# Second expert stage of a four-layer kernel: gelu kept in PSUM, the guard read from PSUM by VectorE, the expert sum on GpSimd in three of four chunks

## The chip, the cores and the metric

The kernel runs on one core of a Trainium2 chip. The time is device microseconds (us) of one execution. Three executions of the kernel before took 1536.53, 1538.46 and 1542.48 us; the median, 1538.46 us, is the figure to be compared. One more execution was taken with the hardware profiler.

## The reference

Four layers run one behind the other on 2 x 1024 = 2048 tokens of width 128, each an attention part and a feed-forward part with a residual and a layer norm around each. The change lies in the last feed-forward part, a mixture of 8 experts of which 2 are weighted for each token:

```python
scores = jax.nn.softmax(inputs @ Wr + br, axis=-1)
_, top_idx = jax.lax.top_k(scores, K)                 # K = 2 of E = 8
mask = jax.nn.one_hot(top_idx, E).sum(-2)
weights = jax.nn.softmax(jnp.where(mask > 0, scores, -jnp.inf), axis=-1)
hid = jax.nn.gelu(jnp.einsum('btc,ecd->bted', inputs, W1) + b1, approximate=False)   # DFF = 512
expert_out = jnp.einsum('bted,edc->btec', hid, W2) + b2
expert_out = jnp.where(jnp.isnan(expert_out), 0.0, expert_out)
return jnp.einsum('bte,btec->btc', weights, expert_out)
```

The line with `isnan` is the guard: a NaN of an expert's output counts as zero. The kernel gets this from max and min against zero (or against the value), which leave every other number as it is. After this part, `x = x + layernorm(...)` gives the output.

## The kernel before

Each of the five engines has one program, written out in order; semaphores hold them together. Nothing is scheduled by a planner: an instruction waits at its place, and everything behind it on its engine waits too. Activations lie transposed, features on the 128 partitions and tokens along the free axis, in four chunks of 512 tokens (`NC = 4`, `CH = 512`).

The second expert stage ("stage 7" in the names) runs over 128 steps: chunk c = i // 32 and m = i % 32, where m counts the quarters (128 hidden features) of the eight experts, four quarters to an expert. I call the four steps of an expert in a chunk a group, n = i // 4, so there are 32 groups, eight in a chunk. fp32 accuracy comes from splitting each number into a rounded part and a rest and multiplying three ways, so every product costs three matmuls. At its loop index i, each engine does this:

- TensorE (`pe_moe7`): three matmuls of the first product of step i into one of four PSUM banks (L2036 to L2038), then three matmuls of the second product of step i - 4 (`LAG7 = 4`; L2042, L2043, L2045). The second products of a group add up in PSUM bank 3 or 4, by turns. Before the first matmul of a group n goes into that bank, TensorE waits until what read group n - 2 out of it is done (semaphore "ye").
- ScalarE (`act_moe7`): gelu of step i from PSUM into an SBUF buffer GE7 (L2485, "ge"), then the rounded copy of step i - 1 (L2491, "hi"); every fourth index the finished group out of its bank with the bias added, into YE7 (L2497, "ye").
- VectorE (`dve_moe7`): the rest of step i, gelu minus its rounded copy (L2560, "lo"), and then one of four stations of group n, station k at index i = 4n + 9 + k. They are the guard's max (L2536, "ca"), its min and sum (L2541, "cb"), the weighting with the token weights (L2549, "cc") and the sum over experts (L2552, "acc").
- GpSimd: splits the weights into the two parts in chunk 0 (L2003, L2005), forms the rests of the stage's input (L2031), and does the small norm steps.
- SyncE: brings the token weights of each group in, broadcast to all partitions.

Beside the steps stand other pieces at fixed (c, m): four feature blocks and their products of the attention before (chunk 0), norm, turning and routing of the second half of the tokens (chunk 1, `dve_route7_*`, `act_route7`), and the final norm of finished chunks (`dve_end` and its parts in chunks 2 and 3).

Names to follow: `hm` counts first products, `w2` second products; `RING7 = 5` buffers hold the rounded part and the rest. In the trace KS and SHARED are SBUF memory (GE7 lies in both), ROUNDED is SBUF with rounded numbers, PS is PSUM.

Of the kernel before, what the change touches and what calls it, by code (L numbers as in the profile page):

```python
# [2993 lines left out]
```

## Time and profile before

| | |
|---|---|
| median of three executions | 1538.46 us |
| the profiled execution | 1548.84 us, its span 1547.0 us |
| mean granted TensorE clock | 0.886 of full speed |
| busy over the span | TensorE 1269.9 us (82%), VectorE 1174.2 (76%), ScalarE 1118.9 (72%), GpSimd 278.8 (18%) |
| second expert stage | first step at 1301.3 us, last first product at 1527.7, end of the span 1547.0 |

The profiled execution is slower than the median by 10.4 us; durations and positions below are its own. A row of a window tells what an engine was busy with, and "idle before" what it waited for. Matmuls overlap in the pipeline: each lasts 0.39 us in the trace, though in the stage's steps they start every 0.23 us at the full clock, so TensorE's pace is read from starts.

### The profile page before, as it was taken

How to read it: one execution, taken by the hardware profiler on the slowest of the kernel's cores; microseconds unless marked ns; L12 is line 12 of the kernel's file. 1: busy time of each engine (PE TensorE's matmuls, PEld its weight loads, DVE VectorE, ACT ScalarE, POOL GpSimd, SP SyncE). 2: the span in 40 equal slices, each digit the busy share in tenths (PEclk: the TensorE clock that was granted, in tenths of full speed). 3: DMA queues.
4: the chain of work that ended last, by engine and by line, in shares of the span. 5: the costliest groups of instructions: out<-in, count | busy, mean ns of one | idle time of the engine just before them, and what ended most of it. 6: DMA issues, size and time to landing. Idle time of an engine off the chain costs nothing.

```text
span 1547.0 us, 22272 instructions
## 1 busy us (share of the span) xinstructions
PE 1269.9 (82%) x8010; PEld 645.8 (42%) x8010; DVE 1174.2 (76%) x2121; ACT 1118.9 (72%) x1584; POOL 278.8 (18%) x377
## 2 busy tenths in 40 slices
PE   6699999986777777777777787788899988788996
PEld 3334444452111111111111145556667766576874
DVE  7878886367697797966669556668978797876898
ACT  4267787658999999999999733455565655967985
POOL 2500002451000000002000034444011035621000
PEclk9589999995788778888788897999999998999998
DMA  5300100004000000100000020013233234001111
GB/s 186 109 23 24 44 24 4 1 11 140 0 21 21 1 21 1 36 21 1 21 1 0 29 116 0 1 25 89 91 99 99 80 103 151 21 28 35 42 48 55
DMA packets 41086, 70.47 MB, mean 46 GB/s; under 512 B 6416, under 2 KB 14864, under 8 KB 40208
## 3 DMA queue, kind: packets, MB, share of 16 engines
q1 hardware_dynamic: 40976, 69.05, 14.5%
q8 instruction: 63, 1.03, 0.3%
q14 instruction: 47, 0.39, 0.1%
HBM read 59.26 MB, written 9.76 MB: 45 GB/s over the span
## 4 chain that ended last, share of the span: by engine, by line
PE 37%; DVE 24%; ACT 20%; issue 13%; POOL 3%; DMA 1%; SPq 1%; DVEq 0%; ACTq 0%; POOLq 0%
ACT SHARED L1134 12%; PE PS L823 5%; DVE SHARED L1170 4%; PE PS L1048 4%; PE PS L1035 3%; PE PS L787 3%; DVE KS L2218 3%; PE PS L645 2%; PE PS L1349 2%; PE PS L712 2%; ACT ROUNDED L2142 2%; PE PS L2036 2%; PE PS L2038 2%; PE PS L2037 1%; PE PS L2045 1%
## 5 line engine op out<-in xcount | busy, mean ns | idle before, releaser
L1134 ACT ACTIVATE SHARED<-PS 128x1536 f32<-128x1536 f32 (+1 forms) x346 | 458.4, 1432 | 34.2 <-PE PS L1035 32.8
L1035 PE MATMUL PS<-QS,KS 48*128 48x512 bf16 (+1 forms) x1006 | 237.2, 461 | 123.4 <-ACT SHARED L1134 118.9
L1170 DVE TENSOR_TENSOR SHARED<-SHARED 128x1536 f32<-128x1536 f32 (+1 forms) x170 | 276.5, 1700 | 45.8 <-ACT SHARED L1134 45.8
L803 ACT ACTIVATE SHARED<-PS 128x512 f32<-128x512 f32 (+3 forms) x384 | 163.8, 493 | 75.4 <-PE PS L791 65.9
L1035 PEld LDWEIGHTS PS<-QS,KS 48*128 48x128 bf16 (+1 forms) x1006 | 40.5, 99 | 365.8 <-ACT SHARED L1134 337.9
L1048 PE MATMUL PS<-SHARED,Vg 128*16 128x512 f32 x1024 | 157.3, 692 | 5.2 <-DVE SHARED L1170 5.1
L2036 PE MATMUL PS<-ROUNDED 128*128 128x512 f32 x328 | 135.8, 414 | 6.2 <-ACT KS L2154 6.2
L732 DVE TENSOR_REDUCE NM<-PS 128x2 f32<-128x1024 f32 (+3 forms) x128 | 124.4, 1019 | 16.0 <-PE PS L718 13.7
L2038 PE MATMUL PS<-ROUNDED 128*128 128x512 f32 x328 | 130.3, 397 | 0.0
L2037 PE MATMUL PS<-ROUNDED 128*128 128x512 f32 x328 | 130.2, 397 | 0.0
L2142 ACT ACTIVATE ROUNDED<-KS 128x512 fp32r<-128x512 f32 x100 | 63.1, 631 | 90.2 <-DVE KS L2218 90.1
L328 POOL TENSOR_SCALAR VEY<-MVY 128x4 f32<-128x4 f32 x32 | 8.9, 279 | 611.2 <-DVE MVY L269 610.5
L2045 PE MATMUL PS<-ROUNDED 128*128 128x512 f32 x228 | 94.1, 413 | 28.2 <-DVE ROUNDED L2200 16.1
L2560 DVE TENSOR_TENSOR ROUNDED<-KS,ROUNDED 128x512 fp32r<-128x512 f32 x103 | 75.1, 732 | 32.1 <-ACT ROUNDED L2491 31.2
L823 PE MATMUL PS<-SHARED,Vg 128*16 128x256 f32 (+3 forms) x1152 | 93.6, 399 | 6.4 <-issue 4.8
L2042 PE MATMUL PS<-ROUNDED 128*128 128x512 f32 x228 | 91.5, 401 | 8.2 <-ACT ROUNDED L2491 4.4
L478 POOL COPY Vg<-XH 128x256 f32<-128x256 f32 x16 | 9.1, 572 | 485.8 <-PE PS L1048 291.4
L2485 ACT ACTIVATE KS<-PS,C 128x512 f32<-128x512 f32 x103 | 71.1, 690 | 27.6 <-PE PS L2038 26.5
L2043 PE MATMUL PS<-ROUNDED 128*128 128x512 f32 x228 | 90.1, 395 | 0.0
L712 PE MATMUL PS<-SHARED 48*128 48x512 bf16 (+3 forms) x384 | 79.3, 364 | 12.8 <-DVE NM L732 6.8
L787 PE MATMUL PS<-SHARED 50*128 50x512 bf16 (+3 forms) x384 | 84.0, 343 | 4.4 <-ACT SHARED L803 2.8
L2200 DVE TENSOR_TENSOR ROUNDED<-KS,ROUNDED 128x512 fp32r<-128x512 f32 x100 | 75.0, 750 | 11.9 <-ACT ROUNDED L2142 7.4
(276 smaller groups left out, 2371.9 us busy)
## 6 DMA issues: line engine op xcount, KB each, us to landing
SHARED<-wx SPq DMA_DIRECT2D x64, 256.0 KB, 3.2
SHARED<-in_moe SPq DMA_DIRECT2D x3, 1600.0 KB, 10.7
SHARED<-wx SPq DMA_DIRECT2D x16, 224.0 KB, 3.0
SHARED<-kx SPq DMA_DIRECT2D x32, 96.0 KB
KS<-kx SPq DMA_DIRECT2D x32, 96.0 KB
SHARED<-wx SPq DMA_DIRECT2D x16, 192.0 KB, 2.9
SHARED<-wx SPq DMA_DIRECT2D x16, 160.0 KB, 2.8
qx<-SHARED SPq DMA_DIRECT2D x16, 128.0 KB, 2.4
```

Source lines behind the costliest of these rows:

```text
L712: ins = pe.matmul(PS[:, slot(k, x):slot(k, x) + n], q[r, p, qt * P:qt * P + P], key[r, p, hi * CH:hi * CH + n], start=True, stop=not diag)
L732: dve.tensor_reduce(out=dst, in_=src, axis=AX.X, op=ALU.max, negate=True).then_inc(A[0, "a_red"], 1)
L787: ins = pe.matmul(bank(at, q0), K0[g % 3][r, p, kt * P:kt * P + P], Q0[g % 3][r, p, qh * CH + q0:qh * CH + CH], start=True, stop=not diag)
L803: act.activation(PB[t % 3][:, h, q0:CH], bank(RING0[n % 3], q0), ACT.Exp, scale=SCORE_SCALE)\
L823: ins = pe.matmul(PS[32 * h:32 * h + VC, 6 * CH + a:6 * CH + b], Vg[g % 2][:, kt, h, :], PB[t % 3][:, h, a:b], start=kt == 0, stop=last an ...
L1035: ins = pe.matmul(bank((v % 2) * GRP + f - a), KS[g % 2][r, h // 2, kt * P:kt * P + P], QS[g % 2][r, h // 2, qh * CH:(qh + 1) * CH], start ...
L1048: ins = pe.matmul(PS[32 * h:32 * h + VC, 6 * CH:7 * CH], Vg[g % 2][:, kt, h, :], EX[:, f * CH:f * CH + CH], start=kt == 0, stop=kt == KT - 1)
L1134: act.activation(dst, PS[:, (v % 2) * GRP * CH:((v % 2) * GRP + b - a) * CH], ACT.Exp if second == qh else ACT.Sigmoid, scale=SCORE_SCALE)\
L1170: dve.tensor_tensor(ex_tile(j), ex_tile(j), GR[w % RING][:, 0:(b - a) * CH], ALU.mult)\
L2036: pe.matmul(dst, w[0], x[0], start=start, stop=False)
L2037: pe.matmul(dst, w[0], x[1], start=False, stop=False)
L2038: return pe.matmul(dst, w[1], x[0], start=False, stop=stop)
```

## The change

Four edits, all in this stage:

1. The gelu is written back into the PSUM bank it came from, and the rounded copy (ScalarE) and the rest (VectorE) read it there. The buffers GE7 are gone. TensorE now gets a first-product bank back when the rest is formed ("lo") and no longer when the gelu is done ("ge").
2. ScalarE's copy of the finished group with its bias (YE7) is gone. VectorE's two guard instructions read the bank directly and add the bias themselves: max(y + b, 0), then min(y + b, that).
3. So TensorE gets a second-product bank back from the second guard instruction ("cb") of group n - 2.
4. In chunks 1 to 3 the weighting and the sum over experts are done on GpSimd (`pool_moe7`), in chunk 0 still on VectorE. The two rests of the input (`pool_rest_of_h`) and the root of the final norm (`pool_y`) stand between them.

```diff
         def pool_from_moe5(pool, pw):
...
-            for c in range(2, 4):
-                pool_rest_of_h(pool, 7, c)
-            for c in range(NC):
-                pool_y(pw, edges["end"], c)
+            pool_moe7(pool, pw)
...
             # pe_moe7, second(i): n, k = divmod(i, 4)
                 pe.wait_ge(A[7, "hi"], i + 1)
                 if k == 0:
                     if n >= 2:
-                        pe.wait_ge(A[7, "ye"], n - 1)
+                        pe.wait_ge(A[7, "cb"], n - 1)
...
                     if i >= len(HM7):
-                        pe.wait_ge(A[7, "ge"], i - len(HM7) + 1)
+                        pe.wait_ge(A[7, "lo"], i - len(HM7) + 1)
...
         def act_moe7(act):
-            for i in range(N7 + 5):
+            for i in range(N7 + 1):
                 c, m = divmod(i, M7)
                 if i < N7:
                     act.wait_ge(A[7, "hm"], i + 1)
-                    if i >= RING7:
-                        act.wait_ge(A[7, "lo"], i - RING7 + 1)
-                    act.activation(GE7[i % RING7], bank(HM7[i % len(HM7)]), ACT.Gelu, bias=col("eb1", m)).then_inc(A[7, "ge"], 1)
+                    act.activation(hidden_bank7(i), hidden_bank7(i), ACT.Gelu, bias=col("eb1", m)).then_inc(A[7, "ge"], 1)
                 if 1 <= i < N7 + 1:
...
-                    act.activation(HG7[n % RING7], GE7[n % RING7], ACT.Copy).then_inc(A[7, "hi"], 1)
-                if i % 4 == 0 and 8 <= i:
...
-                    act.activation(YE7[n % 2], bank(3 + n % 2), ACT.Identity, bias=col("eb2", n % E3))\
-                       .then_inc(A[7, "ye"], 1)
+                    act.activation(HG7[n % RING7], hidden_bank7(n), ACT.Copy).then_inc(A[7, "hi"], 1)
...
+        def weigh7(eng, n):
+            c, e = divmod(n, E3)
+            eng.wait_ge(A[7, "cb"], n + 1)
+            eng.wait_ge(*weights_landed7(n))
+            if n >= 2:
+                eng.wait_ge(A[7, "acc"], summed(n - 1))
+            dst = chunk(ACC7, c) if e == 0 else CC7
+            eng.tensor_tensor(dst, CB7, WB7[n % len(WB7)], ALU.mult).then_inc(A[7, "cc"], 1)
+
+        def gather7(eng, n):
+            c, e = divmod(n, E3)
+            eng.wait_ge(A[7, "cc"], n + 1)
+            eng.tensor_tensor(chunk(ACC7, c), chunk(ACC7, c), CC7, ALU.add).then_inc(A[7, "acc"], 1)
+
+        def pool_moe7(pool, pw):
+            for n in range(E3, E3 * NC):
+                weigh7(pool, n)
+                if n % E3:
+                    gather7(pool, n)
+                if n in (E3 + 1, E3 + 2):
+                    pool_rest_of_h(pool, 7, n - E3 + 1)
+                if n in (17, 18, 25):
+                    pool_y(pw, edges["end"], (17, 18, 25).index(n))
+            pool_y(pw, edges["end"], 3)
...
             # dve_moe7, station(n, k)
-                    dve.tensor_scalar(CA7, YE7[n % 2], 0.0, None, ALU.max).then_inc(A[7, "ca"], 1)
+                    dve.tensor_scalar(CA7, bank(3 + n % 2), col("eb2", e), 0.0, ALU.add, ALU.max)\
+                       .then_inc(A[7, "ca"], 1)
...
-                    dve.scalar_tensor_tensor(out=CB7, in0=YE7[n % 2], scalar=0.0, in1=CA7,
-                                             op0=ALU.min, op1=ALU.add).then_inc(A[7, "cb"], 1)
...
+                    dve.scalar_tensor_tensor(out=CB7, in0=bank(3 + n % 2), scalar=col("eb2", e), in1=CA7,
+                                             op0=ALU.add, op1=ALU.min).then_inc(A[7, "cb"], 1)
+                elif c == 0 and k == 2:
+                    weigh7(dve, n)
+                elif c == 0 and e:
+                    gather7(dve, n)
...
-                    dve.tensor_tensor(HL7[k], GE7[k], HG7[k].bitcast(F32), ALU.subtract).then_inc(A[7, "lo"], 1)
+                    dve.tensor_tensor(HL7[k], hidden_bank7(i), HG7[k].bitcast(F32), ALU.subtract).then_inc(A[7, "lo"], 1)
```

What stands in each engine's row: first TensorE at the last index of chunk 3 that begins a group's second products, before. S7_ge, S7_ye, S7_hi and S7_lo are the semaphores named above.

```order
L2036 MATMUL PS<-ROUNDED 128x512 [waits S7_ge]
L2037 MATMUL PS<-ROUNDED 128x512
L2038 MATMUL PS<-ROUNDED 128x512
L2042 MATMUL PS<-ROUNDED 128x512 [waits S7_ye,S7_hi]
L2043 MATMUL PS<-ROUNDED 128x512
L2045 MATMUL PS<-ROUNDED 128x512 [waits S7_lo]
```

The same place in the change:

```order
L2036 MATMUL PS<-ROUNDED 128x512 [waits S7_lo]
L2037 MATMUL PS<-ROUNDED 128x512
L2038 MATMUL PS<-ROUNDED 128x512
L2042 MATMUL PS<-ROUNDED 128x512 [waits S7_cb,S7_hi]
L2043 MATMUL PS<-ROUNDED 128x512
L2045 MATMUL PS<-ROUNDED 128x512 [waits S7_lo]
```

TensorE's instructions and their order are the same; only two of its waits are for other semaphores.

Then VectorE over one group in chunk 3, before: four rests, and a station behind each.

```order
L2560 TENSOR_TENSOR ROUNDED<-KS,ROUNDED 128x512 [waits S7_w2,S7_hi]
L2536 TENSOR_SCALAR SHARED<-SHARED 128x512 [waits S7_cb,S7_ye]
L2560 TENSOR_TENSOR ROUNDED<-KS,ROUNDED 128x512 [waits S7_w2,S7_hi]
L2541 SCALAR_TENSOR_TENSOR SHARED<-SHARED 128x512 [waits S7_cc,S7_ca]
L2560 TENSOR_TENSOR ROUNDED<-SHARED,ROUNDED 128x512 [waits S7_w2,S7_hi]
L2549 TENSOR_TENSOR SHARED<-SHARED 128x512 [waits S7_acc,w5_in2,S7_cb]
L2560 TENSOR_TENSOR ROUNDED<-KS,ROUNDED 128x512 [waits S7_w2,S7_hi]
L2552 TENSOR_TENSOR SHARED<-SHARED 128x512 [waits S7_cc]
```

The same in the change, where L2569 is the rest, L2550 and L2556 the guard, C the columns with the biases:

```order
L2569 TENSOR_TENSOR ROUNDED<-PS,ROUNDED 128x512 [waits S7_w2,S7_hi]
L2550 TENSOR_SCALAR SHARED<-PS,C 128x512 [waits S7_cb,S7_w2]
L2569 TENSOR_TENSOR ROUNDED<-PS,ROUNDED 128x512 [waits S7_w2,S7_hi]
L2556 SCALAR_TENSOR_TENSOR SHARED<-PS,C,SHARED 128x512 [waits S7_cc,S7_ca]
L2569 TENSOR_TENSOR ROUNDED<-PS,ROUNDED 128x512 [waits S7_w2,S7_hi] x3
```

The guard kept its places in VectorE's row, each behind the rest of its step; the stations for the weighting and the sum are gone.

Last GpSimd's row where the final norm of chunks 0 and 1 begins in the change (weighting L2522, sum L2527):

```order
L2522 TENSOR_TENSOR SHARED<-SHARED 128x512 [waits S7_acc,w5_in0,S7_cb]
L2527 TENSOR_TENSOR SHARED<-SHARED 128x512 [waits S7_cc]
L328 TENSOR_SCALAR VEY<-MVY 128x4 [waits y_var]
L329 TENSOR_TENSOR RSY<-VEY,ROOT 128x4 [waits pw_own]
L2522 TENSOR_TENSOR SHARED<-SHARED 128x512 [waits S7_acc,w5_in2,S7_cb]
L2527 TENSOR_TENSOR SHARED<-SHARED 128x512 [waits S7_cc]
```

Before, L328 and L329 stood there alone; now each pair waits behind the weighting and the sum of a group.

## Rows read from the trace of the kernel before

**Rows 1.** Windows, the stage's four chunks: start:end, length, busy (count), clock, DMA share, GB/s
```profile
core 0: us, PE busy (x) PEld busy (x) DVE busy (x) ACT busy (x) POOL busy (x), PEclk, DMA share, GB/s
1301.30:1371.70 70.40, 59.80 (x247) 44.28 (x246) 49.66 (x79) 57.35 (x97) 33.42 (x33) 0.96 0.10 30
1371.70:1436.80 65.10, 53.92 (x223) 41.35 (x222) 47.96 (x136) 48.65 (x81) 16.99 (x20) 0.92 0.11 33
1436.80:1484.20 47.40, 45.43 (x201) 36.60 (x200) 42.70 (x92) 41.88 (x74) 3.20 (x4) 1.00 0.14 40
1484.20:1527.60 43.40, 42.91 (x191) 35.21 (x190) 39.80 (x78) 40.21 (x71) 1.60 (x2) 1.00 0.16 49
```
**Rows 2.** One line, first products of the stage: count, ns min/median/max, first and last start
```profile
L2036 PE MATMUL PS<-ROUNDED x128: 387/389/799, 1301.3 to 1527.7; 128*128 128x512 f32 x128
```
**Rows 3.** Timeline, an undisturbed group of chunk 3: start, duration, engine, line, operation, names
```profile
1493.74 0.39 PE L2036 MATMUL PS<-ROUNDED 128*128 128x512 f32 x1
1494.62 0.69 ACT L2485 ACTIVATE KS<-PS,C 128x512 f32<-128x512 f32 x1
1495.10 0.39 PE L2036 MATMUL PS<-ROUNDED 128*128 128x512 f32 x1
1495.21 0.62 ACT L2491 ACTIVATE ROUNDED<-KS 128x512 fp32r<-128x512 f32 x1
1495.78 0.39 PE L2042 MATMUL PS<-ROUNDED 128*128 128x512 f32 x1
1495.86 0.69 DVE L2560 TENSOR_TENSOR ROUNDED<-KS,ROUNDED 128x512 fp32r<-128x512 f32 x1 [0.17 <-ACT ROUNDED L2491]
...
1496.47 0.69 DVE L2541 SCALAR_TENSOR_TENSOR SHARED<-SHARED 128x512 f32<-128x512 f32 x1
```
**Rows 4.** Timeline, a wait of TensorE for VectorE in chunk 2
```profile
1476.63 0.39 PE L2043 MATMUL PS<-ROUNDED 128*128 128x512 f32 x1
1478.38 0.50 PE L2045 MATMUL PS<-ROUNDED 128*128 128x512 f32 x1 [1.36 <-DVE ROUNDED L2560]
1478.72 0.40 PE L2036 MATMUL PS<-ROUNDED 128*128 128x512 f32 x1
...
1477.64 0.68 DVE L2560 TENSOR_TENSOR ROUNDED<-KS,ROUNDED 128x512 fp32r<-128x512 f32 x1
```
**Rows 5.** One line each, ScalarE's rounded copies: count, ns min/median/max, first and last start
```profile
L2491 ACT ACTIVATE ROUNDED<-KS x103: 612/630/672, 1304.9 to 1529.7; 128x512 fp32r<-128x512 f32 x103
...
L373 ACT ACTIVATE ROUNDED<-PS x8: 588/591/618, 1022.3 to 1401.3; 128x512 fp32r<-128x512 f32 x8
```
**Rows 6.** One line each, VectorE and GpSimd while weights are split, 1280 to 1300
```profile
L2218 DVE TENSOR_TENSOR KS<-SHARED,PS x7: 674/678/682, 1281.4 to 1296.5; 128x512 f32<-128x512 f32 x7
...
L2200 DVE TENSOR_TENSOR ROUNDED<-KS,ROUNDED x8: 686/882/1750, 1280.8 to 1297.9; 128x512 fp32r<-128x512 f32 x8
...
L2005 POOL TENSOR_TENSOR ROUNDED<-SHARED,ROUNDED x4: 1262/1438/1799, 1288.2 to 1299.5; 128x512 fp32r<-128x512 f32 x4
```
**Rows 7.** One line, VectorE's rests, 1318 to 1341 (chunk 0)
```profile
L2560 DVE TENSOR_TENSOR ROUNDED<-KS,ROUNDED x9: 676/1092/1772, 1317.8 to 1340.9; 128x512 fp32r<-128x512 f32 x9
```
**Rows 8.** Timeline, GpSimd and TensorE in chunk 1
```profile
1387.80 1.74 POOL L340 TENSOR_SCALAR XN<-X,NMX,RSX 128x128 f32<-128x128 f32 x4
...
1392.28 5.00 POOL L340 TENSOR_SCALAR XN<-X,NMX,RSX 128x128 f32<-128x128 f32 x4
...
1397.33 1.12 PE L399 MATMUL PS<-ident,XN 128*128 128x128 f32 x4 [3.47 <-POOL XN L340]
...
1399.10 0.63 PE L2038 MATMUL PS<-ROUNDED 128*128 128x512 f32 x1
1399.53 0.63 PE L2042 MATMUL PS<-ROUNDED 128*128 128x512 f32 x1
```
**Rows 9.** Waits, 1436.8 to 1528 (chunks 2 and 3): who <- whom, us, times, longest
```profile
PE PS L2045 <- DVE ROUNDED L2560: 2.4, 3, 1.4
```
**Rows 10.** Timeline, a turning on TensorE and a norm's statistics on VectorE in chunk 2
```profile
1457.25 0.60 PE L2051 MATMUL PS<-ident,SHARED 128*128 128x128 f32 x4
1457.61 0.47 PE L2036 MATMUL PS<-ROUNDED 128*128 128x512 f32 x1
...
1464.10 0.89 DVE L266 BATCH_NORM_STATS2 STY<-PS 128x6 f32<-128x128 f32 x4
1465.02 0.38 DVE L269 BATCH_NORM_AGGREGATE MVY<-STY 128x2 f32<-128x6 f32 x4
```
**Rows 11.** Windows, the expert stage before, 1140 to 1160
```profile
1140.00:1160.00 20.00, 17.04 (x75) 13.32 (x74) 14.70 (x25) 13.77 (x24) 0.00 (x0) 1.00 0.30 87
```
**Rows 12.** Timeline, the end of the last group
```profile
1531.74 0.50 PE L2045 MATMUL PS<-ROUNDED 128*128 128x512 f32 x1
1532.28 0.69 ACT L2497 ACTIVATE SHARED<-PS,C 128x512 f32<-128x512 f32 x1 [1.43 <-PE PS L2045]
...
1537.35 0.69 DVE L2552 TENSOR_TENSOR SHARED<-SHARED 128x512 f32<-128x512 f32 x1
1538.10 1.11 PE L2051 MATMUL PS<-ident,SHARED 128*128 128x128 f32 x4 [5.86 <-DVE SHARED L2552]
```

More of the change, by code:

```diff
@@ L2301, in pool_split7 @@
             pool_split_weights(pool, 7, 2 * e + 1, M3B[:, k], M3BH[:, k], M3BL[:, k])
-        for nm in ("hm", "ge", "hi", "lo", "w2", "ye", "ca", "cb", "cc", "acc", "lgs"):
+        for nm in ("hm", "ge", "hi", "lo", "w2", "ca", "cb", "cc", "acc", "lgs"):
             A[7, nm] = sem(f"S7_{nm}")
@@ L2308, in sandwich @@
         HM7 = (0, 1, 2, 5)
-        GE7 = [spare[:, 512 * i:512 * i + 512] for i in range(4)] + [arena(2560, 512)]
         HG7 = [rounded(512 * i, 512) for i in range(RING7)]
         HL7 = [work_rounded(512 * i, 512) for i in (0, 1, 2, 3, 9)]
-        YE7 = [work(2048 + 512 * i, 512) for i in range(2)]
         CA7 = work(3072, 512)
@@ L2432, in pe_moe7 @@
                     if i >= len(HM7):
-                        pe.wait_ge(A[7, "ge"], i - len(HM7) + 1)
+                        pe.wait_ge(A[7, "lo"], i - len(HM7) + 1)
                     at = slice(m * P, m * P + P)
-                    pe_parts(pe, bank(HM7[i % len(HM7)]), (M3AH[:, at], M3AL[:, at]), (chunk(hR, c), chunk(HTL[7], c)),
+                    pe_parts(pe, hidden_bank7(i), (M3AH[:, at], M3AL[:, at]), (chunk(hR, c), chunk(HTL[7], c)),
                              True, True).then_inc(A[7, "hm"], 1)
@@ L2476, in pe_beside_moe7, with hidden_bank7 @@
                 pe_turn_y(pe, edges["end"], 2, ACC7, A[7, "acc"], summed(3 * E3 - 1))
+        def hidden_bank7(i):
+            return bank(HM7[i % len(HM7)])
         def act_moe7(act):
-            for i in range(N7 + 5):
+            for i in range(N7 + 1):
                 c, m = divmod(i, M7)
@@ L2531, in station @@
                 if k == 0:
-                    dve.wait_ge(A[7, "ye"], n + 1)
+                    dve.wait_ge(A[7, "w2"], 4 * n + 4)
                     if n:
                         dve.wait_ge(A[7, "cb"], n)
-                    dve.tensor_scalar(CA7, YE7[n % 2], 0.0, None, ALU.max).then_inc(A[7, "ca"], 1)
+                    dve.tensor_scalar(CA7, bank(3 + n % 2), col("eb2", e), 0.0, ALU.add, ALU.max)\
+                       .then_inc(A[7, "ca"], 1)
                 elif k == 1:
@@ L2540, in station @@
                         dve.wait_ge(A[7, "cc"], n)
-                    dve.scalar_tensor_tensor(out=CB7, in0=YE7[n % 2], scalar=0.0, in1=CA7,
-                                             op0=ALU.min, op1=ALU.add).then_inc(A[7, "cb"], 1)
-                elif k == 2:
-                    dve.wait_ge(A[7, "cb"], n + 1)
-                    dve.wait_ge(*weights_landed7(n))
-                    if n >= 2:
-                        dve.wait_ge(A[7, "acc"], summed(n - 1))
-                    dst = chunk(ACC7, c) if e == 0 else CC7
-                    dve.tensor_tensor(dst, CB7, WB7[n % len(WB7)], ALU.mult).then_inc(A[7, "cc"], 1)
-                elif e:
-                    dve.wait_ge(A[7, "cc"], n + 1)
-                    dve.tensor_tensor(chunk(ACC7, c), chunk(ACC7, c), CC7, ALU.add).then_inc(A[7, "acc"], 1)
+                    dve.scalar_tensor_tensor(out=CB7, in0=bank(3 + n % 2), scalar=col("eb2", e), in1=CA7,
[4 more added lines that the diff above has]
+                    gather7(dve, n)
             for i in range(N7 + 9):
```

4 lines of the change are left out of this document (removed).

## The prediction, on record before the changed kernel ran

> **What bounds the kernel now.** I read the windows of the stage first, since all edits lie in it. Each chunk has 32 steps of six matmuls. Undisturbed, a step takes 1.36 us, as two first products in a row show (1493.74 and 1495.10, [rows 3]), 0.23 a matmul, so 32 steps take 43.5 us. Chunk 3 takes about that, and chunk 2 takes 47.4 [rows 1]: TensorE sets the pace there and the others keep up. Chunks 0 and 1 take 70.4 and 65.1: TensorE stands waiting for ScalarE and VectorE, which have the attention pieces, the norms and the routing beside the steps. Then I read the waits of chunks 2 and 3: TensorE's for the rests add up to 2.4 us [rows 9]. So relief for ScalarE and VectorE is worth next to nothing in the second half of the stage, and a new wait of TensorE is paid there in full.
>
> Last I read the timeline of one undisturbed group, for how far each engine lies behind TensorE [rows 3]. First product 103 starts at 1493.74 and its gelu 0.88 later. The rounded copy of step 102 follows at 1495.21, the rest of step 102 at 1495.86, and the guard's second instruction at 1496.47; it ends at 1497.16. That instruction belongs to group 23, because "cb" of group n' stands behind the rest of step 4n' + 10.
>
> **The new wait, and its price.** In the change the first matmul of group n's second products waits for "cb" of group n - 2. TensorE issues it at its index 4n + 4. "cb" of n - 2 stands in VectorE's row behind the rest of step 4n + 2. That rest needs rounded copy 4n + 2, which stands on ScalarE behind gelu 4n + 3, and that needs first product 4n + 3, issued one index (1.36 us) earlier. The chain closes within one index: TensorE can't run ahead of it, and idle time of the others doesn't loosen it. Before, ScalarE's bias copy gave the bank back.
>
> The trace of before shows the size, since both ends stand in it: group 25's second products begin at 1495.78, and "cb" of group 23 ends at 1497.16 [rows 3], 1.38 us too late. To this come:
> - 0.06 from the end of a VectorE instruction to the matmul it releases (1477.64 + 0.68 = 1478.32, matmul at 1478.38, [rows 4]);
> - 0.11 for the restart: behind a wait the next matmul follows at 0.34 instead of 0.23 (1478.38 to 1478.72, [rows 4]);
> - less 0.04, since the rounded copy now reads PSUM, 0.591 instead of 0.630 [rows 5].
>
> No row shows a gelu that writes PSUM. Its nearest row is the same gelu into SBUF, which lets the copy behind it start 0.59 later (1494.62 to 1495.21, [rows 3]). I keep that, and take 0.10 less and 0.10 more as bounds, which is how far a gelu and a copy of the same shape lie apart (0.69 and 0.59, [rows 3, 5]). A VectorE instruction with one input in PSUM took 0.678 [rows 6], against 0.69 for the rest and the guard now [rows 3]: no change. The sum is 1.51 us a group, 1.4 to 1.6.
>
> The Trainium skill, PSUM, section Specifications (TRN2), says that ScalarE writes faster to PSUM than to SBUF. No row here shows such a write. By it the wait would lie at its lower end.
>
> Chunks 2 and 3 have eight such groups each (TensorE's indices 64 to 124): 16 x 1.51 = 24.2. Against it, most of the stalls that the final norms cause now go away, because VectorE, busy 39.80 of 43.40 us in chunk 3 [rows 1], loses two of eight instructions and gets longer groups (6.95 us). These stalls are what stands above the steps: from index 64 (1436.8) to 127 (1527.7, [rows 1, 2]) 90.9, less 63 x 1.36 = 85.7, less three turnings of 0.4 (1457.25 to 1457.61, [rows 10]) = 4.0. But the statistics, 1.3 us ahead of a guard [rows 10], still delay "cb" by some 0.5, three times. Chunks 2 and 3: 24.2 - 4.0 + 1.5 = +21.7.
>
> **The bank freed by "lo" in place of "ge".** Undisturbed, the rest of a step ends 4.2 after its first product (copy, rest: 1496.55 - (1493.74 - 1.36), [rows 3]), and the product that waits for it starts four indices, 5.4, after. This wait hides, but where VectorE is behind it can cost up to 1 us, once or twice.
>
> **Chunk 0.** Beside GpSimd's splitting, a VectorE instruction with two SBUF inputs stretched to 1.750, while one with an SBUF and a PSUM input stayed at 0.674 to 0.682 in the same 20 us [rows 6]. In chunk 0 the rests stand at a median of 1.092 and reach 1.772 [rows 7]; with an input in PSUM they would return to 0.68, some 0.5 less each over the dozen of that stretch. The Trainium skill, SBUF, section Who interferes with whom, says just this: two SBUF inputs contend with a GpSimd instruction that reads SBUF, one does not. But ScalarE is the fullest of the three there (57.35 of 70.4, [rows 1]) and loses only eight bias copies of 0.69 [rows 12]. Against that stand the new waits of six groups; a feature block on ScalarE hides some, in the last two or three groups nothing does. Relief bounds the gain at 5, four bare waits (4 x 1.5, less 2 of relief) the loss at 4. I take 0.
>
> **Chunk 1.** Gains: GpSimd's second block of L340 took 5.00 where the first took 1.74, beside VectorE's rests with two SBUF inputs; TensorE waited 3.47 for it and then ran at 0.43 a matmul instead of 0.23 [rows 8], which is the lower clock. Together 3.5 + some 12 matmuls x 0.2 = 6. Losses: eight new waits, 12, of which two or three with norm or routing pieces in front of the guard are longer by 1.5, less what the chunk's other 21.6 us of waiting already cover; I take half of these 16, 8. Net +2, from -5 to +6.
>
> **GpSimd.** A weighting and a sum take 2 x 1.26 (the unstretched 1262, [rows 6]) in a group of 6.95 us, and VectorE has hardly an instruction with two SBUF inputs left to collide with. It keeps up: "cc" of n - 1 is there long before "cb" of n needs it.
>
> **The end.** The last first product starts at t = 1527.7 [rows 2]. Then the matmul that waits for "cb" of group 29 goes at t + 3.4 (0.88 + 0.59 + 0.59 to the rest 126, 0.61 + 0.69 to the guard's end, and 0.06) instead of t + 1.36, and eleven more start by t + 6.0, where they did by t + 4.0 (1531.74, [rows 12]). Before, a backlog of stations brought the turning to t + 10.4 (1538.10, [rows 12]). Now VectorE starts 0.54 behind the last matmul, as ScalarE does in [rows 12]; two guard instructions of 0.7 and two of GpSimd of 1.26, each with a release of about 0.06, follow in series: 6.0 + 0.5 + 1.5 + 2.7 = 10.7, and 11.1 if GpSimd is still at the group before. I take +0.6. The Trainium skill, GPSIMD Engine Reference, section 4.1 Engine selection, has GpSimd at about twice VectorE's time for two-input elementwise work: the trace, 1.26 against 0.69, agrees.
>
> **The sum.** +21.7 (chunks 2 and 3) + 0 + 2 + 0.6 = +24.3. The profiled execution would go from 1548.84 (span 1547.0, 1.84 around it) to 1573.1. The median of the runs stands 10.4 below it, so 1538.5 + 24.3 = 1562.8.
>
> **Rivals.**
> - The wait is covered and the stage gets faster. For it: ScalarE loses 32 x 0.69 = 22 us, VectorE 45 instructions of 0.69, 31 us, and the contention in chunk 0. Then the 4.0 of stalls in chunks 2 and 3, 5 in chunk 0 and 6 in chunk 1 would go: 1538.5 - 15 + 1 = 1524. It decides where "cb" of n - 2 ends 1.4 us sooner after first product 4n + 3 than in the trace. Against it: in [rows 3] the chain holds hardly any queueing, so relief shortens nothing in it. Chance 0.04.
> - The waits of chunks 2 and 3 come as forecast, but the first two chunks gain some 18, both loaded engines being relieved: 1538.5 + 22 - 18 = 1543. Against it: ScalarE's load in chunk 0. Chance 0.07.
> - The regular waits pull the granted clock down. It had means of 0.96 and 0.92 in chunks 0 and 1, with their long waits [rows 1]. Against it: in the expert stage before, TensorE was busy 17.04 of 20 and kept 1.00 [rows 11]. If every third wait brought ten matmuls at 0.43, each would lose 2: +10, so 1573. Chance 0.12.
> - GpSimd is later than reckoned and "cb" waits for "cc" (a pair would have to take 6 us, not 2.5): 1580 or more. Chance 0.03.
> - The forecast: 0.74, its own range 1553 to 1571.
>
> A measurement can tell about 0.5%, 7.7 us, from no change. Faster than 1530.8: 0.05. Within: 0.06. Slower than 1546.2: 0.89. The range holds the forecast's bounds (chunks 0 and 1 by -12 to +8 around their terms, the sixteen waits by 1.6, the end by 1) and most of the clock's case: 1550 to 1574.
>
> **What would show it.** The waits of chunks 2 and 3 name TensorE's L2042 behind VectorE's second guard instruction (L2556), once a group, some 1.4 us each. The chunks take 57 and 55 us, at a clock of 1.00. VectorE's rests stand at 0.68 throughout chunk 0. I am wrong if L2042 does not wait there, or if chunks 0 and 1 together shrink by over 10 us.

## The result, and the profile after

The changed kernel took 1590.73 us (median of four executions, 1589.01 to 1591.63), the kernel before 1538.62 (four, 1536.53 to 1542.48). The ratio is 1.0331, with a 95% interval of 1.0308 to 1.0355. By the medians the change is 52.1 us slower. The direction was forecast; the size was not: 24.3 us were forecast, and the time lies above the range.

The profiled execution took 1591.46 us, its span is 1589.5. Its windows of the four chunks answer to [rows 1], with the same columns:

```profile
1294.30:1373.10 78.80, 62.74 (x247) 47.39 (x246) 41.84 (x79) 54.14 (x91) 27.47 (x33) 0.90 0.09 27
1373.10:1452.70 79.60, 60.87 (x223) 47.26 (x222) 49.92 (x126) 43.55 (x73) 23.39 (x29) 0.83 0.08 27
1452.70:1511.90 59.20, 47.25 (x201) 36.04 (x200) 39.88 (x78) 37.98 (x66) 21.77 (x19) 1.00 0.11 37
1511.90:1568.50 56.60, 45.11 (x192) 34.62 (x191) 35.90 (x63) 36.49 (x63) 20.55 (x17) 1.00 0.13 38
```

Chunk 0 is 8.4 us longer, chunk 1 14.5, chunk 2 11.8, chunk 3 13.2. ScalarE is busy for less in every chunk and VectorE in all but chunk 1, as the edits promise, and the stage is longer all the same. With the end (21.0 after the last first product, before 19.3) the stage is 49.7 us longer, nearly the 52.1 of the medians. The spans differ by less, 42.5, because the stage begins at 1294.3 here and at 1301.3 before, though the program up to it is the same: the profiled execution of before took 10.4 us more than the median, and its stage begins later than in any other profiled execution here (1287.0 to 1295.3).

**Chunks 2 and 3.** The waits from 1452.7 to 1568.5 (who <- whom, us, times, longest) answer to [rows 9]:

```profile
POOL SHARED L2522 <- DVE SHARED L2556: 67.9, 16, 6.5
...
PE PS L2042 <- DVE SHARED L2556: 21.7, 15, 2.1
```

TensorE waits for VectorE's second guard instruction once a group, 1.4 us on average (a sixteenth such wait, 1.35 us, stands in the view under a ScalarE copy). GpSimd stands waiting for the guard 67.9 of 115.8 us, and no guard waits for it there. One group of chunk 2, beside [rows 3]; its chain begins one index earlier, with the first product at 1503.33:

```profile
1504.33 0.66 ACT L2482 ACTIVATE PS<-PS,C 128x512 f32<-128x512 f32 x1 [0.60 <-PE PS L2038]
...
1504.82 0.39 PE L2036 MATMUL PS<-ROUNDED 128*128 128x512 f32 x1
...
1504.91 0.59 ACT L2488 ACTIVATE ROUNDED<-PS 128x512 fp32r<-128x512 f32 x1
...
1505.53 0.69 DVE L2569 TENSOR_TENSOR ROUNDED<-PS,ROUNDED 128x512 fp32r<-128x512 f32 x1 [0.41 <-ACT ROUNDED L2488]
...
1506.14 0.74 DVE L2556 SCALAR_TENSOR_TENSOR SHARED<-PS,C,SHARED 128x512 f32<-128x512 f32 x1
...
1507.03 0.47 PE L2042 MATMUL PS<-ROUNDED 128*128 128x512 f32 x1 [1.37 <-DVE SHARED L2556]
...
1507.80 0.40 PE L2036 MATMUL PS<-ROUNDED 128*128 128x512 f32 x1
```

This is the chain of the prediction, link by link: gelu, rounded copy, rest, guard, matmul. The guard ends at 1506.14 + 0.74 = 1506.88, and the matmul that it releases starts at 1507.03. From one first product to the next it is 2.98 us instead of 1.36, so the wait costs 1.62. It was put at 1.51, within 1.4 to 1.6; the guard's instruction lasts 0.742 where 0.69 was taken, and 0.15 instead of 0.06 lies between its end and the matmul. The gelu into PSUM changed nothing here: the copy starts 0.58 behind it, where 0.59 was taken.

**Chunk 1.** Here the same wait is longer. TensorE, then VectorE in the same stretch:

```profile
1379.17 0.39 PE L2038 MATMUL PS<-ROUNDED 128*128 128x512 f32 x1
1383.22 0.77 PE L2042 MATMUL PS<-ROUNDED 128*128 128x512 f32 x1 [3.66 <-DVE SHARED L2556]
1383.78 0.63 PE L2043 MATMUL PS<-ROUNDED 128*128 128x512 f32 x1
...
1388.90 0.53 PE L2043 MATMUL PS<-ROUNDED 128*128 128x512 f32 x1
1389.27 0.39 PE L2045 MATMUL PS<-ROUNDED 128*128 128x512 f32 x1
```

```profile
1379.35 0.88 DVE L266 BATCH_NORM_STATS2 STY<-PS 128x6 f32<-128x128 f32 x4
1380.27 0.38 DVE L269 BATCH_NORM_AGGREGATE MVY<-STY 128x2 f32<-128x6 f32 x4
1380.57 0.86 DVE L266 BATCH_NORM_STATS2 STY<-PS 128x6 f32<-128x128 f32 x4
1381.46 0.38 DVE L269 BATCH_NORM_AGGREGATE MVY<-STY 128x2 f32<-128x6 f32 x4
1381.75 0.66 DVE L2569 TENSOR_TENSOR ROUNDED<-PS,ROUNDED 128x512 fp32r<-128x512 f32 x1
1382.33 0.74 DVE L2556 SCALAR_TENSOR_TENSOR SHARED<-PS,C,SHARED 128x512 f32<-128x512 f32 x1
```

The norm's statistics (2.4 us) stand in VectorE's row ahead of the rest and the guard; the whole burst is handed to TensorE. Behind the wait thirteen matmuls last 0.58 or more and follow each other at 0.43 us instead of 0.23: TensorE's clock is at the lower of its two levels, 1.2 GHz. The Trainium skill, TensorE: Matmul & The Clock Gate, Part 1, says that the clock follows how busy TensorE has been; the trace agrees, with a mean of 0.83 in this chunk. The chunk has eight waits over 0.3 us, 18.7 us together (before, six in the stage's own matmuls, 7.0, and two more ahead of others, 4.2, one of them the 3.47 of [rows 8]), and 50 of its 192 stage matmuls last 0.58 or more (before 18). At 0.2 us each the 32 more slow matmuls explain 6.4 of the 14.5, and the longer waits 7.5.

**Chunk 0.** The same, by way of ScalarE. The profile names different releasers, but all four waits of L2042 there (4.23, 1.32, 2.96 and 1.31 us) end 0.10 to 0.11 after L2556 does. The longest:

```profile
1318.98 1.28 ACT L1754 ACT_TABLE_LOAD   x1
...
1321.23 1.28 ACT L2482 ACT_TABLE_LOAD   x1
1322.53 0.66 ACT L2482 ACTIVATE PS<-PS,C 128x512 f32<-128x512 f32 x1
1323.11 0.59 ACT L2488 ACTIVATE ROUNDED<-PS 128x512 fp32r<-128x512 f32 x1
...
1323.73 0.69 DVE L2569 TENSOR_TENSOR ROUNDED<-PS,ROUNDED 128x512 fp32r<-128x512 f32 x1 [3.38 <-ACT ROUNDED L2488]
1324.16 0.61 ACT L2488 ACTIVATE ROUNDED<-PS 128x512 fp32r<-128x512 f32 x1
1324.34 0.74 DVE L2556 SCALAR_TENSOR_TENSOR SHARED<-PS,C,SHARED 128x512 f32<-128x512 f32 x1
...
1325.18 0.77 PE L2042 MATMUL PS<-ROUNDED 128*128 128x512 f32 x1 [4.23 <-ACT ROUNDED L2488]
```

VectorE is idle here and ScalarE comes late, from an attention piece (L1754 to L1759, with a table load of its own) and the load of gelu's table. The row names L2488, but the last such copy ended at 1324.77; the guard ended at 1325.08. Three more waits of this chunk stand at the first products, behind rests (L2036 for L2569: 1.99, 3.08 and 0.41 us). They come from "lo" in place of "ge" and aren't what the chunk lost: e3 and e1 below have the first two as well (1.97 and 3.10, 2.05 and 3.13), and take 73.0 and 70.3 us in chunk 0.

**What the edits themselves do** (one row each: count, ns min/median/max). VectorE's rests from 1294 to 1345, beside [rows 7]; then gelu, rounded copy and GpSimd's weighting over the stage:

```profile
L2569 DVE TENSOR_TENSOR ROUNDED<-PS,ROUNDED x18: 657/691/693, 1299.7 to 1344.7; 128x512 fp32r<-128x512 f32 x18
...
L2482 ACT ACTIVATE PS<-PS,C x128: 623/662/717, 1295.9 to 1569.4; 128x512 f32<-128x512 f32 x128
...
L2488 ACT ACTIVATE ROUNDED<-PS x128: 570/591/664, 1297.8 to 1570.4; 128x512 fp32r<-128x512 f32 x128
...
L2522 POOL TENSOR_TENSOR SHARED<-SHARED x24: 1262/1288/1296, 1403.6 to 1578.0; 128x512 f32<-128x512 f32 x24
```

The rests are back at 0.69 beside the splitting, where they had reached 1.772.

**The end**, beside [rows 12]; the last first product starts at 1568.48:

```profile
1572.06 0.47 PE L2042 MATMUL PS<-ROUNDED 128*128 128x512 f32 x1 [2.06 <-DVE SHARED L2556]
...
1573.53 0.63 PE L2042 MATMUL PS<-ROUNDED 128*128 128x512 f32 x1
...
1575.66 0.63 PE L2045 MATMUL PS<-ROUNDED 128*128 128x512 f32 x1
...
1580.61 1.12 PE L2051 MATMUL PS<-ident,SHARED 128*128 128x128 f32 x4 [4.31 <-POOL SHARED L2527]
```

The wait ends at t + 3.6 (forecast t + 3.4), but the matmuls from 1573.53 run at the lower clock, so the last starts at t + 7.2 (forecast 6.0) and the turning at t + 12.1 (forecast 11.1).

### The profile page after: what moved, and what is told of

Its sections match the earlier page's. It is cut to its first block, busy times and chain, and to the rows that moved or that the text cites. A ratio compares the mean times of both kernels' runs of the same rounds, so it can differ in the third digit from the quotient of the medians.

```text
span 1589.5 us, 22087 instructions
## 1 busy us (share of the span) xinstructions
PE 1274.2 (80%) x8010; PEld 650.9 (41%) x8010; DVE 1157.4 (73%) x2076; ACT 1101.1 (69%) x1552; POOL 324.5 (20%) x422
## 4 chain that ended last, share of the span: by engine, by line
PE 37%; DVE 24%; ACT 21%; issue 14%; POOL 2%; SPq 1%; DMA 1%; DVEq 0%; POOLq 0%; ACTq 0%
ACT SHARED L1134 11%; DVE SHARED L1170 5%; PE PS L823 4%; PE PS L1048 4%; PE PS L1035 3%; PE PS L787 3%; DVE KS L2218 3%; PE PS L645 2%; PE PS L1349 2%; PE PS L2042 2%; PE PS L2036 2%; PE PS L2038 2%; PE PS L2037 2%; PE PS L712 2%; ACT ROUNDED L2142 1%
## 5 line engine op out<-in xcount | busy, mean ns | idle before, releaser
L2569 DVE TENSOR_TENSOR ROUNDED<-PS,ROUNDED 128x512 fp32r<-128x512 f32 x128 | 87.4, 687 | 104.3 <-ACT ROUNDED L2488 103.6
L2482 ACT ACTIVATE PS<-PS,C 128x512 f32<-128x512 f32 x128 | 85.0, 664 | 100.4 <-PE PS L2038 100.3
L2036 PE MATMUL PS<-ROUNDED 128*128 128x512 f32 x328 | 139.0, 424 | 13.2 <-DVE ROUNDED L2569 6.8
L2042 PE MATMUL PS<-ROUNDED 128*128 128x512 f32 x228 | 96.3, 423 | 56.2 <-DVE SHARED L2556 41.3
L2037 PE MATMUL PS<-ROUNDED 128*128 128x512 f32 x328 | 132.8, 405 | 0.0
L2038 PE MATMUL PS<-ROUNDED 128*128 128x512 f32 x328 | 132.6, 404 | 0.0
L328 POOL TENSOR_SCALAR VEY<-MVY 128x4 f32<-128x4 f32 x32 | 7.7, 242 | 502.5 <-DVE MVY L269 501.8
L2045 PE MATMUL PS<-ROUNDED 128*128 128x512 f32 x228 | 94.6, 415 | 16.3 <-DVE ROUNDED L2200 16.2
L2043 PE MATMUL PS<-ROUNDED 128*128 128x512 f32 x228 | 92.8, 407 | 0.0
L712 PE MATMUL PS<-SHARED 48*128 48x512 bf16 (+3 forms) x384 | 77.9, 359 | 14.5 <-DVE NM L732 7.0
L2200 DVE TENSOR_TENSOR ROUNDED<-KS,ROUNDED 128x512 fp32r<-128x512 f32 x100 | 75.0, 750 | 11.9 <-ACT ROUNDED L2142 7.4
```

Source lines behind the costliest of these rows:

```text
L2036: pe.matmul(dst, w[0], x[0], start=start, stop=False)
L2037: pe.matmul(dst, w[0], x[1], start=False, stop=False)
L2038: return pe.matmul(dst, w[1], x[0], start=False, stop=stop)
L2042: pe.matmul(dst, w[0], x[0], start=start, stop=False)
```

## The experiments

Three theories stood against each other. The bank's wait: TensorE must wait for "cb", and that is the whole loss. "lo" in place of "ge": the first products wait for the rests. GpSimd: its two instructions are slow, or late for somebody. The table has all profiled executions, cut at first products 0, 32, 64, 96 and 127 and the end of the span, in us; "stage" is their sum. The medians are of 4 to 29 executions. Each ratio is against the kernel before on the same chip, so kernels from different chips are compared by their ratios. Chunk 0 varies by up to 4 us between profiled executions of one kernel (73.6 and 69.7, 70.3 and 72.2); the others by less than 1.5.

| kernel | chunk 0 | 1 | 2 | 3 | end | stage | median | ratio |
|---|---|---|---|---|---|---|---|---|
| before | 70.4 | 65.1 | 47.4 | 43.4 | 19.3 | 245.6 | 1538.4 to 1540.6 | |
| after | 78.9 | 79.6 | 59.2 | 56.6 | 21.0 | 295.3 | 1590.7 | 1.0331 [1.0308, 1.0355] |
| e1_guard_3_earlier | 70.3 | 62.7 | 48.4 | 44.4 | 19.1 | 244.9 | 1541.9 | 1.0010 [0.9989, 1.0031] |
| e2_guard_only | 76.1 | 79.6 | 61.3 | 57.2 | 20.2 | 294.4 | 1587.8 | 1.0314 [1.0280, 1.0347] |
| e3_gelu_only | 73.0 | 59.6 | 48.4 | 44.5 | 19.3 | 244.8 | 1537.4 | 0.9993 [0.9970, 1.0017] |
| e4_gpsimd_only | 71.5 | 67.2 | 47.8 | 44.0 | 22.5 | 253.0 | 1549.1 | 1.0063 [1.0038, 1.0088] |
| e5_pieces_behind_guard | 78.8 | 77.4 | 60.2 | 56.5 | 20.7 | 293.6 | 1589.0 | 1.0327 [1.0305, 1.0349] |
| e6_guard_1_earlier | 72.3 | 63.7 | 50.4 | 47.0 | 19.4 | 252.8 | 1545.1 | 1.0045 [1.0027, 1.0062] |
| e7_guard_early_only | 73.6 | 62.6 | 48.0 | 43.5 | 18.9 | 246.6 | 1533.5 | 0.9966 [0.9947, 0.9985] |
| e8_all_but_gpsimd_early | 70.3 | 60.4 | 48.8 | 44.5 | 18.0 | 242.0 | 1535.7 | 0.9976 [0.9961, 0.9992] |
| e9_guard_1_later | 96.1 | 97.6 | 86.9 | 80.7 | 22.3 | 383.6 | 1679.4 | 1.0897 [1.0871, 1.0923] |
| e10_guard_2_earlier | 71.7 | 59.2 | 48.7 | 44.5 | 19.2 | 243.3 | 1535.4 | 0.9969 [0.9948, 0.9991] |
| e11_guard_early_only_again | 69.7 | 61.2 | 47.7 | 43.5 | 18.8 | 240.9 | 1536.9 | 0.9981 [0.9968, 0.9994] |
| e12_all_but_gpsimd_again | 72.2 | 60.5 | 48.8 | 44.5 | 18.0 | 244.0 | 1536.3 | 0.9975 [0.9959, 0.9991] |

**e1_guard_3_earlier.** The changed kernel with all of VectorE's stations three indices earlier, so that "cb" of n - 2 stands well ahead of where TensorE asks for it:

```diff
-            for i in range(N7 + 9):
+            for i in range(N7 + 6):
...
-                if 9 <= i:
-                    station((i - 9) // 4, (i - 9) % 4)
+                if 6 <= i:
+                    station((i - 6) // 4, (i - 6) % 4)
```

> The changed kernel with one number moved: VectorE does station k of group n at its index 4n + 6 + k instead of 4n + 9 + k, so the guard's second instruction comes three steps (4.1 us) earlier and still behind its inputs. Theory G (the loss is the wait of TensorE for cb, closed within one index): the sixteen waits of chunks 2 and 3 are gone (a step is 1.36 us throughout), chunks 2 and 3 take 45 and 44 us instead of 59.2 and 56.6, and chunks 0 and 1, if their 23 us of loss hang on the same wait, go back to 70 and 65 or less: 1525 to 1540 us. Theory L (in chunks 0 and 1 it is the first-product bank given back by lo): chunks 2 and 3 recover 27, chunks 0 and 1 stay at 79 and 80: about 1563. Theory P (GpSimd's share is at fault): 1580 or more.

With one number changed the stage is back at 244.9 us, 50 less, and the ratio can't be told from 1 (the median of 1541.9 is 2 above the expected stretch). In the waits of chunks 2 and 3 no row of TensorE's L2042 is left; what TensorE still waits for is this:

```profile
PE PS L2036 <- DVE ROUNDED L2569: 4.3, 3, 2.1
```

**e2_guard_only.** The kernel before with ScalarE's copy of the finished group taken out and the guard reading the bank. Gelu in SBUF, weighting and sum on VectorE:

```diff
-                        pe.wait_ge(A[7, "ye"], n - 1)
+                        pe.wait_ge(A[7, "cb"], n - 1)
...
-                if i % 4 == 0 and 8 <= i:
-                    n = (i - 8) // 4
...
-                    act.activation(YE7[n % 2], bank(3 + n % 2), ACT.Identity, bias=col("eb2", n % E3))\
-                       .then_inc(A[7, "ye"], 1)
...
-                    dve.wait_ge(A[7, "ye"], n + 1)
+                    dve.wait_ge(A[7, "w2"], 4 * n + 4)
```

> The kernel before with only the bias copy taken out and the guard reading the bank, so that TensorE waits for cb; gelu in SBUF, the weighting and the sum on VectorE everywhere. Theory G: chunks 2 and 3 lose 12 to 13 us each and chunks 0 and 1 lose too: 1580 to 1600, since VectorE carries more here than in the change. Theory L: chunks 2 and 3 as in G, chunks 0 and 1 as before: about 1563. Theory P: near 1538.

This edit alone costs 49.4 us by the medians, where the whole change costs 52.1. Its waits in the whole stage (1288.7 to 1583):

```profile
PE PS L2042 <- DVE SHARED L2535: 46.7, 24, 4.5
```

**e3_gelu_only.** The kernel before with gelu kept in PSUM and the first-product bank returned by "lo":

```diff
-                        pe.wait_ge(A[7, "ge"], i - len(HM7) + 1)
+                        pe.wait_ge(A[7, "lo"], i - len(HM7) + 1)
...
-                    act.activation(GE7[i % RING7], bank(HM7[i % len(HM7)]), ACT.Gelu, bias=col("eb1", m)).then_inc(A[7, "ge"], 1)
+                    act.activation(hidden_bank7(i), hidden_bank7(i), ACT.Gelu, bias=col("eb1", m)).then_inc(A[7, "ge"], 1)
```

> The kernel before with only the gelu kept in PSUM (first-product bank given back by lo, no buffers for the gelu). Theory G: a little faster or the same, 1530 to 1540, the rests in chunk 0 at 0.69 us beside GpSimd's splitting. Theory L: chunks 0 and 1 lose some 20: about 1558.

No change that can be measured: the theory of "lo" falls as a cause. It gives chunk 1 5.5 us (no slow matmuls are left there), as the prediction had it for the relief of GpSimd's L340, and takes 1 each in chunks 2 and 3, where TensorE waits 4.3 us for the rests at L2036.

**e4_gpsimd_only.** The kernel before with the weighting and the sum on GpSimd in chunks 1 to 3:

```diff
-                elif k == 2:
-                    dve.wait_ge(A[7, "cb"], n + 1)
...
+                elif c == 0 and k == 2:
+                    weigh7(dve, n)
+                elif c == 0 and e:
+                    gather7(dve, n)
```

> The kernel before with only the weighting and the sum of chunks 1 to 3 on GpSimd. Theory G: VectorE is relieved but its rests and guard keep two SBUF inputs and now meet GpSimd's two instructions of 1.3 us a group: 1532 to 1550. Theory P: 1560 or more, with TensorE waiting for rests stretched beyond 1 us.

A loss of its own, 10.7 us by the medians and 7.4 by the stage. 3.2 of it stand at the end, where three pairs remain to be done in series and TensorE waits for the last (second profile below). The weighting on GpSimd, over the stage (first profile), is one sign of a collision: beside VectorE's rests with two SBUF inputs its median is 1.674 us, and 1.288 in the changed kernel, where those read PSUM. The rests reach 1.820 us in the other direction. How much of the other 4.2 us this makes is not shown.

```profile
L2529 POOL TENSOR_TENSOR SHARED<-SHARED x24: 1263/1674/1845, 1389.4 to 1534.2; 128x512 f32<-128x512 f32 x24
```

```profile
1536.85 1.12 PE L2051 MATMUL PS<-ident,SHARED 128*128 128x128 f32 x4 [8.56 <-POOL SHARED L2534]
```

The Trainium skill, SBUF — State Buffer, section Who interferes with whom, has VectorE's second pair of ports shared with GpSimd; the two medians agree. The loss doesn't add to the guard's: e2 and the changed kernel differ by 3 us.

**e5_pieces_behind_guard.** The changed kernel with two of VectorE's pieces in chunk 1 moved from ahead of a guard's second instruction to behind it:

```diff
-            if c == 1 and m == 1:
+            if c == 1 and m == 2:
                 dve_y(dve, own, edges[7], 2)
...
-            if c == 1 and m == 21:
+            if c == 1 and m == 22:
                 dve_route7_b(dve, own, 1)
```

> The changed kernel with two pieces of VectorE in chunk 1 one index later, so that they stand behind the guard's second instruction and not in front of it: the statistics of two chunks (2.4 us, from index 33 to 34) and the second routing piece (from 53 to 54). Theory S (in chunks 0 and 1 the wait for cb costs more than its bare 1.6 us because pieces stand in its closed chain, and because waits over about 3 us are followed by a dozen matmuls at 0.43 us instead of 0.23): the wait before matmul group 37 falls from 3.7 to about 1.5 us and the slow matmuls behind it go, the one before 57 likewise, 5 to 9 us in all: 1582 to 1586. Rival (the loss of chunk 1 comes from somewhere else, as from ScalarE's own pieces): 1589 to 1592.

A miss in size. TensorE in chunk 1:

```profile
1378.64 0.47 PE L2042 MATMUL PS<-ROUNDED 128*128 128x512 f32 x1 [1.38 <-DVE SHARED L2556]
...
1385.06 0.50 PE L2036 MATMUL PS<-ROUNDED 128*128 128x512 f32 x1 [1.41 <-DVE ROUNDED L2569]
...
1390.59 0.76 PE L2042 MATMUL PS<-ROUNDED 128*128 128x512 f32 x1 [4.58 <-DVE SHARED L2556]
```

The wait of 3.66 fell to the bare 1.38, and the matmul at its end lasts 0.47 instead of 0.77, so the burst was what stretched it. But behind it one of 1.41 is new, and the next one grew from 3.29 to 4.58: the piece was only handed to the next link. The second piece did the same: 3.75 fell to 1.80, and the wait behind it grew from 2.64 to 3.94, with a new one of 1.02 ahead of it. Added up, the chunk's waits over 0.3 us didn't fall at all (19.6 us, before 18.7); its slow matmuls fell from 50 to 31, which at 0.2 us is 3.8 us. Chunk 1 won 2.2 us, the median 1.7: what was won is clock, not waiting.

**e6_guard_1_earlier**, **e10_guard_2_earlier** and **e9_guard_1_later.** The edit of e1 with 8, 7 and 10 in place of 9: where the wait begins to hurt.

> The changed kernel with each station of VectorE one index earlier (4n + 8 + k). The wait for cb then closes over two indices: of the bare 1.6 us a group 1.36 are covered and about 0.3 stay. Theory G: chunks 2 and 3 take about 50 and 46 us, chunks 0 and 1 are back to within 5 us of the kernel before: 1545 to 1555. If the cost were a fixed price of any wait on a VectorE semaphore (rival), it would stay near 1590.

> The changed kernel with each station two indices earlier (4n + 7 + k): the bare wait is covered whole (1.6 less 2.7). Theory G: as e1, 1538 to 1545, chunks 2 and 3 at 48 and 44 us. Together with e6 and e9 this gives the price by place: none, about 0.3, 1.6, 3.0 a group.

> The changed kernel with each station of VectorE one index later (4n + 10 + k). Theory G: the chain now starts from the first product just before the waiting matmul, so each of the sixteen bare waits of chunks 2 and 3 grows by one index, 1.36 us, to about 3.0: a group takes 8.4 us instead of 7.1, chunks 2 and 3 take some 69 and 66, and if waits of 3 us also bring the lower clock (a dozen matmuls at 0.43 us after each), up to 2.5 us more a group. Without the clock 1620 to 1635, with it up to 1675. Rival (a fixed price of the wait, whatever stands in the chain): about 1590.

One index earlier takes away nine tenths of the loss. "cb" then stands one step of 1.36 ahead, which leaves a quarter of a microsecond of the 1.62, and a group of chunk 3 has this (TensorE):

```profile
1492.02 0.39 PE L2038 MATMUL PS<-ROUNDED 128*128 128x512 f32 x1
1492.43 0.47 PE L2042 MATMUL PS<-ROUNDED 128*128 128x512 f32 x1
1492.74 0.40 PE L2043 MATMUL PS<-ROUNDED 128*128 128x512 f32 x1
```

0.41 instead of 0.23, and 0.31 instead of 0.23 behind it. Two indices earlier nothing is left of it, and the kernel is 0.3% faster than before. That is below the expected 1538 to 1545. e1, with the guard one index earlier still, was at 1.0010 on another chip, so these two don't settle whether the changed kernel is then faster than before or the same. One index later the wait is longer by one whole step: TensorE in chunk 3 of e9, and the chunk's window.

```profile
1594.81 0.39 PE L2038 MATMUL PS<-ROUNDED 128*128 128x512 f32 x1
1597.94 0.76 PE L2042 MATMUL PS<-ROUNDED 128*128 128x512 f32 x1 [2.74 <-DVE SHARED L2556]
1598.50 0.63 PE L2043 MATMUL PS<-ROUNDED 128*128 128x512 f32 x1
...
1601.06 0.51 PE L2043 MATMUL PS<-ROUNDED 128*128 128x512 f32 x1
1601.41 0.39 PE L2045 MATMUL PS<-ROUNDED 128*128 128x512 f32 x1
...
1607.96 0.61 PE L2042 MATMUL PS<-ROUNDED 128*128 128x512 f32 x1 [2.74 <-DVE SHARED L2556]
```

```profile
1575.90:1656.60 80.70, 56.65 (x192) 43.25 (x191) 35.07 (x62) 36.55 (x64) 20.39 (x17) 0.83 0.11 33
```

A group takes 10.02 us (1597.94 to 1607.96) instead of 7.09: 1.37 more of waiting, and 1.5 for seven or eight matmuls at the lower clock. Seven of the eight waits in this chunk are such bare ones of 2.74 (the eighth, 4.87, has the norm in it). In the changed kernel the bare wait of 1.37 costs nothing in clock here (mean 1.00); at 2.74 (mean 0.83) the clock adds about half as much again as the wait. By the medians e9 is 88.7 us above the changed kernel, 3.0 for each of the 30 groups that wait for a bank. Its 1679.4 us is above the 1675 that was expected at most: the clock was expected behind waits of 3 us, and waits in chunks 0 and 1 grew to as much as 7.2.

**e7_guard_early_only** and **e8_all_but_gpsimd_early**, and their repetition in five rounds, **e11_guard_early_only_again** and **e12_all_but_gpsimd_again.** e7 has the edits of e2 and this one; e8 has those of e3 as well:

```diff
-            for i in range(N7 + 9):
+            for i in range(N7 + 6):
...
-                if 9 <= i:
-                    station((i - 9) // 4, (i - 9) % 4)
+                if 6 <= i:
+                    station((i - 6) // 4, (i - 6) % 4)
```

> The kernel before with the bias copy taken out and the guard reading the bank, as in e2, but each station three indices earlier; gelu in SBUF, weighting and sum on VectorE. Theory G with the relief of ScalarE (32 instructions of 0.69) real: ScalarE-bound places in chunks 0 and 1 gain 2 to 8 us: 1528 to 1537. Rival (ScalarE's relief is worth nothing, as VectorE sets the pace there): 1537 to 1542.

> As e1 (all edits, stations three indices earlier) but with the weighting and the sum on VectorE in all chunks. If GpSimd's share costs its tail (two instructions of 1.3 us instead of 0.69) and collisions, this is 2 to 8 us faster than e1: 1533 to 1539. If the relief of VectorE is worth more: 1545.

> The same kernel as e7 with more rounds, to see whether its gain of 0.3% holds: 1532 to 1537 expected, ratio 0.996 to 0.998. If it was the chance of one chip, 1.000.

> The same kernel as e8 with more rounds, beside e11 on one chip: which of the two is the better version. Its stage was 4.6 us shorter than e7's in the profiles, its median 2.2 us longer. Expected: ratio 0.996 to 0.999, no difference to e11 that can be told.

Both are faster than before, by 0.2 to 0.3%, 4 to 6 us, with all intervals below 1. So dropping ScalarE's 32 copies and moving the stations forward are together worth this much. The kernel before with its stations moved and nothing else wasn't run, so the share of each isn't shown. Which of e7, e8 and e10 is best can't be told apart.

## Why the prediction was wrong in size

- **The new wait and its chain: right.** It is at L2042, behind L2556, once a group; the chain closes within one index; the clock stays at 1.00 in chunks 2 and 3. e2, e1 and e9 show each alone that it is the cause. Mis-sized: 1.62 instead of 1.51, 1.8 us over sixteen groups.
- **Chunks 2 and 3: +25.0 instead of +21.7.** Beside those 1.8, the three passes of the final norm cost some 2.3 instead of 1.5: in two of them the step with the wait took 3.67 and 3.30 us instead of 2.98, and in three places the first products waited some 0.4 for rests behind the norm's L310, which GpSimd had stretched. The remaining 0.7 is spread over many steps, a few hundredths each.
- **Chunk 0, "I take 0": the first failed step.** It measured +8.5 in this pair of executions. The three kernels with the wait at this place (after, e2, e5) took 78.9, 76.1 and 78.8, mean 77.9, and those without it or with the stations earlier 69.7 to 73.6, mean 71.5, so some 6 is the wait's. The relief of contention came as read (rests at 0.69), and no run shows a gain from it: e3, which has it alone, took 73.0. Attention pieces and table loads of ScalarE stand inside the closed chain; two of the four waits were 4.23 and 2.96 us, and low clock follows (31 slow stage matmuls instead of 10). The prediction allowed four bare waits of 1.5.
- **"lo" in place of "ge", "up to 1 us, once or twice": mis-sized.** Two such waits in chunk 0 took 1.99 and 3.08 us. e1 and e3 have them too and lose nothing by the stage: they stand where other waits stood before.
- **Chunk 1, "Net +2": the step that failed most.** It measured +14.5. The larger part of the miss is the clock: the prediction counted 12 slow matmuls fewer (2.4 us won) and none more behind the new waits, and there were 50 instead of 18 (6.4 us lost), 8.8 us beside the forecast. The smaller part is the waiting. The prediction took 3.5 off for L340, which came true (the second block fell from 5.00 to 2.21 and its wait is gone), and put 8 on, half of the 16 that it gave the new waits, since the other half would hide in 21.6 us of waiting. But of these 21.6, the chunk less 32 steps, only 11.2 were waits; the rest went to other pieces of TensorE and to slow matmuls. The waits grew by 11.0 beside L340's, so 3.0 more than forecast: a burst on VectorE passes to TensorE in its whole length where the chain is closed.
- **The end: +1.7 instead of +0.6**, for matmuls at the lower clock.
- The terms close: 24.3 forecast, and 8.5 + 12.5 + 3.3 + 1.1 more, make 49.7, the stage's difference.
- **The rivals.** Covered waits and a gain in chunks 0 and 1 were both wrong. The clock's rival was wrong where it was put (sixteen regular waits of 1.4 us kept 1.00) and right as a mechanism where the waits are longer, in chunks 0 and 1 and the end. GpSimd was late for a guard only once in the whole stage, by 0.2 us. How chunk 1's loss parts into clock and waiting is counted (slow matmuls times 0.2), not measured by itself. Two pairs bear it out: e5, above, and e1, where with the chain open the chunk's waits are 13.5 us instead of 18.7 and its slow matmuls none instead of 50. That is 5.2 and 10.0 of the 16.9 us between the two.

## What to carry to other kernels

Before a buffer's release moves to a later consumer, write down at which index the producer asks for it, at which it is given back, and what stands between on every engine in the chain: if both meet within one step, everything queued there, bursts too, falls on the producer. Price such a wait with its bursts and with the clock that follows them, not by its bare length. And try the consumer one or two places earlier: here that took a loss of 3.3% away and left ratios of 0.997 to 1.001.
